# A graph, attention and expert layer on one core: order of transfers, of a branch's pieces, and one-hots and mixer operations given to POOL

## What is computed

```
xn  = layernorm(x)
q,k,v = xn @ Wq,Wk,Wv ;  e = edge_attr @ We            (8 heads of 32)
alpha = <q[dst], k[src] + e> / sqrt(32)
w   = softmax of alpha over the edges of one dst
gnn = segment_sum((v[src] + e) * w, dst) + xn @ Wskip
mix = linear attention over all nodes (phi(q) kv / z) @ Wo,
      layernorm, relu(. @ W1) @ W2, layernorm
x   = x + gnn + mix
x   = x + sum over 8 experts of gate * MLP_e(layernorm(x))
```

## Time and profile before

| | us |
|---|---|
| median of 3 runs | 3732.03 |
| lowest, highest | 3723.98, 3732.52 |
| the profiled execution | 3703.33 |
| its span | 3701.4 |
| PE busy | 3241.8 (88%) |
| DVE busy | 2927.2 (79%) |
| ACT busy | 1719.3 (46%) |
| POOL busy | 1259.3 (34%) |

### The profile page before, as it was taken

The page is one execution under the profiler, slowest core; times in us unless marked ns, Lnnn a source line. Parts: engine busy times, 40 slices in busy tenths (PEclk is TensorE's granted clock), DMA queues, the critical chain, the costliest instruction groups (busy, mean ns, idle before and its releaser), DMA issues.

```text
span 3701.4 us, 72350 instructions
## 1 busy us (share of the span) xinstructions
PE 3241.8 (88%) x17312; PEld 2525.9 (68%) x17312; DVE 2927.2 (79%) x6394; ACT 1719.3 (46%) x4685; POOL 1259.3 (34%) x1313
## 2 busy tenths in 40 slices
PE   4998899999999899999999177777768999999999
PEld 3775566666666666666666145555558999999999
DVE  6776898898888888888888888888856666666665
ACT  1222333333333333333333156666646777777776
POOL 1223666666666666666664021111100000000000
PEclk9998999999999999999999599999979999999999
DMA  7336988898888988888888256666610000000000
GB/s 177 116 115 172 243 250 238 234 249 242 243 245 238 245 237 244 244 246 239 245 238 222 91 173 207 206 207 206 207 60 12 12 17 11 17 11 17 11 17 9
DMA packets 520911, 593.54 MB, mean 160 GB/s; under 512 B 187937, under 2 KB 396979, under 8 KB 520319
## 3 DMA queue, kind: packets, MB, share of 16 engines
q1 hardware_dynamic: 312408, 351.02, 32.7%
q0 software_dynamic: 201888, 232.77, 24.1%
q10 hardware_dynamic: 6409, 7.46, 0.6%
HBM read 426.91 MB, written 163.17 MB: 159 GB/s over the span
## 4 chain that ended last, share of the span: by engine, by line
PE 52%; DVE 18%; issue 13%; SPq 5%; DMA 3%; DVEq 3%; ACT 3%; ACTq 2%; another core or an unknown queue 0%
PE psum L635 10%; PE psum L637 10%; PE psum L636 10%; PE psum L713 6%; PE psum L697 5%; DMA region_s<-ab_d 3%; DVE weights L1373 3%; DVE part L1387 3%; PE psum L849 3%; PE psum L770 2%; DVE region_s L1572 2%; DVE region_x L1560 1%; ACTq L1088 1%; ACT region_s L1083 1%; DVEq L1563 1%
## 5 line engine op out<-in xcount | busy, mean ns | idle before, releaser
L600 POOL DMA_INDIRECT weights<-kv_tab,idx x450 | 547.7, 1217 | 351.9 <-ACT idx L1006 192.1
L1012 ACT ACTIVATE weights<-psum,region_s 125x250 f32<-125x250 f32 x450 | 211.7, 471 | 951.2 <-PE psum L713 524.6
L697 PE MATMUL psum<-we,weights 64*125 64x256 f32 x1800 | 578.4, 428 | 6.5 <-issue 3.4
L849 PE MATMUL psum<-region_s 125*125 125x264 f32 x1800 | 453.9, 401 | 128.8 <-DVE region_s L1572 128.8
L713 PE MATMUL psum<-region_x,weights 125*125 x1800 | 546.9, 429 | 0.0
L1129 ACT ACTIVATE region_s<-psum,bns 128x250 f32<-128x250 f32 x800 | 403.4, 555 | 287.2 <-PE psum L637 287.2
L1622 DVE TENSOR_TENSOR parts_h<-region_s,parts_h 128x500 fp32r<-128x500 f32 x400 | 269.9, 679 | 312.4 <-ACT parts_h L1133 283.1
L849 PEld LDWEIGHTS psum<-region_s 125*125 125x125 f32 x1800 | 304.6, 188 | 277.9 <-issue 152.7
L713 PEld LDWEIGHTS psum<-region_x,weights 125*125 125x125 f32 x1800 | 320.3, 198 | 190.2 <-issue 159.6
L600 POOL DMA_INDIRECT kv_more<-kv_tab,idx x300 | 364.2, 1214 | 142.6 <-issue 102.0
L697 PEld LDWEIGHTS psum<-we,weights 64*125 64x125 f32 x1800 | 291.2, 190 | 163.2 <-issue 148.0
(11 more groups left out here) (246 smaller groups left out, 7628.2 us busy)
## 6 DMA issues: line engine op xcount, KB each, us to landing
region_s<-ve_d SPq DMA_DIRECT2D x450, 256.0 KB, 2.9
ve_d<-weights SPq DMA_DIRECT2D x225, 256.0 KB
ve_d<-kv_more SPq DMA_DIRECT2D x150, 256.0 KB
weights<-in_attr_t SPq DMA_DIRECT2D x450, 62.5 KB
ve_d<-region_r SPq DMA_DIRECT2D x75, 256.0 KB
kv_tab<-region_s SPq DMA_DIRECT2D x50, 224.0 KB
region_s<-ab_d SPq DMA_DIRECT2D x450, 1.0 KB
weights<-kv_tab,idx POOLq DMA_INDIRECT x450
```

What stands on the lines that cost most here:

```text
L600: nc.gpsimd.indirect_dma_start(kg[r][0:T, w, :], None, kv_tab, bass.IndirectOffsetOnAxis(idx[:, r, w:w + 1], 0)).then_inc(gathered[r], 16)
L697: last = mm(psum[0:T, s % 2, w * D:(w + 1) * D], att_b[:, s % RP, w * T:(w + 1) * T], we[:, :], start=True, stop=True)
L849: last = mm(bank, hot[:, s, w, :], pv[:, s, w, 0:PV], start=(w == 0), stop=(w == 1))
```

## The change

- SP loads the dst rows of step k+3 in step k (`AHEAD`), as the first thing of the step, ahead of the store and the attribute load; it has a second set of registers for that, loaded every six steps as well. The first three loads stand ahead of the loop.
- PE's `qprod` stands ahead of `eproj` and `spread` in a step. The branch's pieces of PE are placed anew: "attend", "turn" and "out" one step later, "up" at steps 4 to 7 and 9 to 12, and "down" spread over six steps, of which two lie in the next block (`last_at`). "up" of the pairs 1 to 3 uses one PSUM bank, and waits for the relu of the pair just before.
- ACT's pieces move with them. DVE's "attend" stands at step 4, "norm2" at 3.
- DVE's gain1, gain2 and add2 are done by POOL, at steps 1, 9 and 11 of later blocks, with two new semaphores.
- DVE's register loads stand behind the first large operation of their step, in both loops.
- In the sums pass DVE makes the one-hot of step 0, ACT those of 1, 3 and 5, and POOL those of 2 and 4, with one comparison for each of the two tiles.
- Two semaphores are merged into others.

```diff
-BY_DVE = {0: 1, 3: 2}
-BY_ACT = {1: 1, 2: 2, 4: 3, 5: 4}
+BY_DVE = {0: 1}
+BY_ACT = {1: 1, 3: 2, 5: 3}
+BY_POOL = {2: 1, 4: 2}
...
+            sp.load(ab_regs, walk[0:1, 0, 0:SU])
+            for s in range(AHEAD):
+                load_ab(s, s, ab_regs[s])
...
                     if s % SU == 0:
                         sp.load(regs, walk[0:1, 0, bass.ds(k, SU)])
+                        sp.load(ab_regs, walk[0:1, 0, bass.ds(k + AHEAD, SU)])
+                    if k + AHEAD < STEPS:
+                        load_ab(k + AHEAD, (s + AHEAD) % SB, ab_regs[s % SU])
...
-                    load_ab(k, s, regs[s % SU])
...
+            def gain1(b):
+                pool.wait_ge(m_x1, b + 1)
+                nc.gpsimd.tensor_tensor(my[:, b % 2], mx1, row2(R_G1), ALU.mult).then_inc(m_g1, 1)
+            def gain2(b):
+                pool.wait_ge(m_x2, b + 1)
+                order(nc.gpsimd.tensor_tensor(mx2[:, :, :], mx2[:, :, :], row2(R_G2), ALU.mult))
+            def add2(b):
+                pool.wait_ge(m_res_in, (b + 1) * 32)
+                nc.gpsimd.tensor_tensor(mout[:, :, :], mx2[:, :, :], mres[:, :, :], ALU.add).then_inc(m_outr, 1)
...
+                    if s == 1 and b >= 1:
+                        gain1(b - 1)
+                    if s == 9 and b >= 2:
+                        gain2(b - 2)
+                    if s == 11 and b >= 2:
+                        add2(b - 2)
...
+                        order(placed)
+                        for w in range(2):
+                            compared = nc.gpsimd.tensor_scalar(hot[:, s, w, :], iota[:, :], place_in[:, s, w:w + 1], None, ALU.is_equal)
+                        compared.then_inc(hot_pool, 1)
...
-                    if n == 4 and not (isinstance(b, int) and b == NB - 1):
-                        pe.wait_ge(m_an, b + 2)
                     if o == 0 and pair >= 2:
-                        pe.wait_ge(m_hr, b * 4 + pair - 1)
+                        pe.wait_ge(m_hr, b * 4 + pair)
...
-            mix_at = {2: ("q", 0), 3: ("q", 1), 7: ("attend",), 10: ("turn",), 11: ("out", 0), 12: ("out", 1)}
-            late_at = {1: ("turn1",), 3: ("up", 0), 4: ("up", 1), 5: ("up", 2), 6: ("up", 3), 10: ("up", 4), 11: ("up", 5),
-                       12: ("up", 6), 13: ("up", 7), 14: ("down", 0, 3), 15: ("down", 3, 7), 16: ("down", 7, 11), 17: ("down", 11, 16)}
+            mix_at = {2: ("q", 0), 3: ("q", 1), 8: ("attend",), 11: ("turn",), 12: ("out", 0), 13: ("out", 1)}
+            late_at = {1: ("turn1",), 4: ("up", 0), 5: ("up", 1), 6: ("up", 2), 7: ("up", 3), 9: ("up", 4), 10: ("up", 5),
+                       11: ("up", 6), 12: ("up", 7), 14: ("down", 0, 3), 15: ("down", 3, 6), 16: ("down", 6, 9), 17: ("down", 9, 12)}
+            last_at = {0: ("down", 12, 14), 1: ("down", 14, 16)}
...
                     if some:
+                        qprod(k - LAGQ, (s - LAGQ) % SB, regs[s % SU])
                         eproj(k - LAGQ, (s - LAGQ) % SB, b * (SB // RP) + (s - LAGQ) // RP + 1, 0)
...
-                        qprod(k - LAGQ, (s - LAGQ) % SB, regs[s % SU])
...
-            mix_at, late_at = {1: "phi", 8: "turn", 17: "turn1"}, {2: 0, 4: 1, 9: 2, 11: 3}
+            mix_at, late_at = {1: "phi", 9: "turn", 17: "turn1"}, {3: 0, 5: 1, 8: 2, 10: 3}
...
-            mix_at = {0: "phi", 3: "attend", 8: "sum1", 9: "stats1", 10: "root", 11: "root2", 12: "norm1", 13: "gain1"}
+            mix_at = {0: "phi", 4: "attend", 8: "sum1", 9: "stats1", 10: "root", 11: "root2", 12: "norm1"}
             late_at = {15: "sum2", 16: "stats2", 17: "root"}
-            last_at = {1: "root2", 4: "norm2", 5: "gain2", 6: "add2"}
+            last_at = {1: "root2", 3: "norm2"}
...
                     add_edges(k, s, b * (SB // RK) + s // RK + 1)
+                    if s % SU == 0:
+                        dve.load(regs, walk[0:1, 2, bass.ds(k, SU)])
                     multiply(k, s)
```

More of the change, by code:

```diff
@@ L58 @@
 LAGS = 2
+AHEAD = 3
 LAGP = 2
@@ L464, in _ @@
             regs = [sp.alloc_register(f"sp_pair{s}") for s in range(SU)]
+            ab_regs = [sp.alloc_register(f"sp_ab{s}") for s in range(SU)]
             def load_ab(k, s, reg):
@@ L605, in _ @@
                 b_body(b)
+            gain1(NB - 1)
+            for b in (NB - 2, NB - 1):
+                gain2(b)
+                add2(b)
+            order.reset()
             pool.wait_ge(back, CT)
@@ L611, in d_body @@
             def d_body(it):
-                for s in BY_ACT:
+                for s in range(SU):
+                    if s in BY_DVE:
+                        continue
                     k = it * SU + s
@@ L802, in b_body @@
                         eproj(k - LAGQ, (s - LAGQ) % SB, b * (SB // RP) + (s - LAGQ) // RP + 1, 1)
-                        qprod(k - LAGQ, (s - LAGQ) % SB, regs[s % SU])
+                    if s in last_at and not (isinstance(b, int) and b < 2):
+                        mix(b - 2, u, last_at[s])
                     if s in late_at and not (isinstance(b, int) and b == 0):
@@ L815, in _ @@
                 eproj(STEPS - LAGQ + s, SB - LAGQ + s, (STEPS - LAGQ + s) // RP + 1, 1)
-                qprod(STEPS - LAGQ + s, SB - LAGQ + s, regs[s])
-            for g in late_at.values():
+                if s in last_at:
+                    mix(NB - 2, 1, last_at[s])
+            for g in (*late_at.values(), *last_at.values()):
                 mix(NB - 1, 0, g)
@@ L1035, in mix @@
                         n = 2 * pair + o
-                        last = fn(mh[:, n, :], psum[:, 5 + pair % 2, o * BN:(o + 1) * BN], ACT.Relu,
+                        last = fn(mh[:, n, :], psum[:, 5 if pair == 0 else 6, o * BN:(o + 1) * BN], ACT.Relu,
                                   bias=cols[:, C_B1 + n:C_B1 + n + 1])
                     last.then_inc(m_hr, 1)
-            mix_at, late_at = {1: "phi", 8: "turn", 17: "turn1"}, {2: 0, 4: 1, 9: 2, 11: 3}
+            mix_at, late_at = {1: "phi", 9: "turn", 17: "turn1"}, {3: 0, 5: 1, 8: 2, 10: 3}
             def b_body(b, u):
@@ L1421, in mix @@
                 elif g == "norm1":
+                    wait(dve, m_g1, b)
                     signal(norm_apply(my[:, u], mx1), m_x1, b + 1)
-                elif g == "gain1":
-                    order(tt(my[:, u], mx1, row2(R_G1), ALU.mult))
                 elif g == "root":
@@ L1453, in b_body @@
                     k = b * SB + s
-                    if s % SU == 0:
-                        dve.load(regs, walk[0:1, 2, bass.ds(k, SU)])
                     if s in last_at and not (isinstance(b, int) and b < 2):
@@ L1562, in d_body @@
             def d_body(it):
-                dve.load(regs, walk[0:1, 1, bass.ds(it * SU + LAGQ - LAG, SU)])
                 for s in range(SU):
@@ L1573, in d_body @@
                        pv[:, s, :, D:PV].unsqueeze(3).broadcast_to((T, 2, H, C)), ALU.mult).then_inc(pv_ready, 1)
+                    if s == 0:
+                        dve.load(regs, walk[0:1, 1, bass.ds(it * SU + LAGQ - LAG, SU)])
                     if s >= LAG or not (isinstance(it, int) and it == 0):
```

41 lines of the change are left out of this document (24 added, 17 removed).

## The result

| us | before | after |
|---|---|---|
| median (4 runs each, on one chip) | 3732.28 | 3600.72 |
| lowest to highest | 3723.98 to 3742.75 | 3597.34 to 3612.18 |
| profiled execution, its span | 3703.33, 3701.4 | 3612.18, 3610.2 |

The ratio is 0.9652, 95% interval 0.9619 to 0.9684: 132 us less by the medians. The forecast was 3607. The two traces differ by only 91 us, since the profiled execution of before was 21 us under the lowest of its four runs and that of after was the slowest of its four.

The account below looks back on a forecast made before the run. PE and DVE, coupled step by step, were taken to bound the edge stage, DVE the sums pass. Blocks of 63.7 us save 100, iterations of 7.3 save 25: 3732 - 125 = 3607 us, range 3520 to 3692.

Parts of the forecast that it names:

- What bounds the kernel: Edge stage: PE and DVE coupled through two PSUM banks, unequal steps costing more than either sum; sums pass: DVE.
- The first list of pairs: Edge stage before: larger of PE's step s+5 and DVE's step s, added over 18 steps, given as 64.8 us a block.
- Part 1: Edge stage: dst rows three steps sooner are never late; the whole 76.7 us and most of the 29.9 go.
- Part 2: Edge stage: levelled branch brings the pairs to 62.9, 1.9 us less a block; DVE waits up to 2 for "out".
- Part 3: Edge stage: with DVE's register load behind the add, some 2 of 3.2 us of waiting a block go.
- Part 4: Edge stage: three operations on POOL, hidden there, each holding DVE 0.4 us, 1.2 us a block.
- Part 5: Sums pass: one one-hot and part of a load gap leave DVE, comparisons cost 0.47; iteration 7.3 us, 25 us saved.
- A: Edge stage: dst-row load was hidden anyway, only DVE's relief of 51 us comes, sums pass gives nothing: 3681; chance 0.22.
- B: Both stages reach their floors, 60 us a block and 6.83 an iteration: 3482; chance 0.15.
- D: Both stages: the moves cancel (wait at "out", shared bank for "up", comparison near 0.74 us): 3732; chance 0.08.
- C: Both stages: the port decides, POOL operations wait out multiplies and hold DVE, slower: about 3806; chance 0.10.

Follow-up runs that it names:

- edge_only: The changed kernel with the sums pass of before, so only the edge-stage edits: 3675.55 us, ratio to before 0.9860.
- no_level: The changed kernel with PE's old order in a step and the branch's old places: 3597.00 us, ratio to before 0.9658.
- nopm_noload: no_poolmix with DVE's register load of the edge stage ahead of the add again: 3582.67 us, ratio to before 0.9622.
- ahead_sums: The kernel before with only the early dst rows and the two sums-pass edits: 3584.13 us, ratio to before 0.9603.
- store_first: The changed kernel with SP's store ahead of the dst rows and one register load of nine, not two of six: 3606.86 us, ratio to before 0.9689.
- ahead_only: The kernel before with only the dst rows loaded three steps sooner: 3651.13 us, ratio to before 0.9792.
- no_poolmix: The changed kernel with gain1, gain2 and add2 back on DVE: 3560.07 us, ratio to before 0.9567.
- pool_memset: no_poolmix with four POOL memsets, which read no SBUF, in each place of the three operations: 3566.38 us, ratio to before 0.9587.

## Why the prediction was right, step by step

The total was right (125 us foreseen, 132 measured) by terms that made up for each other; that it came within 7 us is luck. The sums pass gave 43 us more than foreseen, the edge stage 50 less. The 100 us of the edge stage were 2.9 us a block for stalls and slow clock (72 us; the dst rows and DVE's register loads share this term), 1.9 for the new positions (48), less 0.8 for the waits that they bring (20). The runs give 60 to 74 for the rows and 16 to 23 for the register load, nothing for the positions, and take 32 to 41 for POOL's operations; edge_only, with all of them, gave 50.

- **What bounds the kernel**: right for the sums pass (DVE), half right for the edge stage. That PE's and DVE's steps pair off, with the larger of each pair as the price, is not borne out. The first list of pairs adds to 64.6 as printed, not 64.8. Recounted from the two lists, some 0.5 of the 1.9 us a block is DVE's relief (the pairs where gain2 and gain1 stood), and levelling alone is 1.2 to 1.4 us, 30 to 35 us in all. Levelling measured nothing twice (no_level against after, nopm_noload against ahead_sums), to within some 20 us.
- **Part 1, dst rows**: the edit was worth what was foreseen, the way was half right. The load is gone from the waits, the spread idles 26.8 us (foreseen under 30), and no price of the second register load shows (store_first). But "the whole 76.7 and most of the 29.9 go" is true of that row only: in all PE idles as long as before (124 and 128 us in before and ahead_only), now for DVE, and the gain in the traces is PE's work at a higher clock. So that 60 to 74 us lie near the 76.7 of the row is in part luck.
- **Part 2, levelling**: the term that failed. The foreseen wait at "out" came (24.3 us) and was free; the 1.9 us a block did not come. The one-hot is ready in time, as foreseen (5.8 us of waiting for ACT against 24.6), but PE waits for DVE instead, before its query. The granted clock is 0.96, short of the 0.98 foreseen.
- **Part 3, DVE's load**: mechanism right, size off. Norm1's 42.4 us of idle time are 0.0; 16 to 23 us came of 50.
- **Part 4, POOL's mixer operations**: the sign was wrong. The hold was priced well: 1.29 us an operation as foreseen, and 35.7 us over the 71 operations up to the last step is 0.50 each where I took 0.4. (The row that it rests on was misread: the DVE operation of the earlier trace rows ends at 73.89, not with POOL's at 73.61. That it took 0.96 us is right.) The prediction let slack between the pairs absorb most of this hold, and that failed; the relief of DVE, 51 us of busy time, was worth next to nothing beside it. That a relief is taken up by the ring and the two banks, while a hold of 2 us falls into one step, is argued and not shown. Why the price (32 to 41 us) is as large as the whole sum of the holds isn't shown. The granted clock differs too, 0.97 with them and 1.00 without in the two inner windows; what part it has is open.
- **Part 5, sums pass**: 68 us for 25. A comparison takes 0.95 us (median) and never less than 0.588. The median lies above my upper end of 0.74, and the least above my 0.35 and the 0.38 estimated beside it. Yet the multiplies are not pushed apart, where I charged 0.47 an iteration. Without that charge my sum was 6.83; measured are 6.79. The overlap took its toll from POOL, which has the time: 395 us busy of 509.
- **Rivals**: A's price fell with ahead_only, though the turn of stalls into waits for DVE is real. B's floor of 6.83 came in the sums pass, its 60 us a block did not: from the first to the last spread a block takes 66.7 us in before, 65.5 in after and 63.4 in no_poolmix. D, the moves cancelling, holds for the edge stage's edits beside the dst rows, not for the whole. C fell; its mechanism (POOL's turn holds DVE) is real in the edge stage and absent in the sums pass.

The edge stage shows DVE's small add ending with POOL's operation every time it was held, and pool_memset shows no hold. The Trainium skill, SBUF — State Buffer, section "SBUF: two separate sides", says as much: a Vector operation with two SBUF inputs and a GpSimd operation that reads SBUF lock each other out, and whichever starts second waits for the whole of the first. The start times of the edge stage do not fit its last part, as 17 of the 30 held adds were recorded as started first. Nor do the sums pass's multiplies: they have two SBUF inputs, POOL's comparisons read SBUF, and only the comparisons were stretched.

## What to carry to other kernels

Before work goes from DVE to POOL, look at which operations of DVE run beside it: beside a two-operand POOL operation a 0.165 us add took up to 2.2 us, while comparisons with one tensor input held nothing in a pass where POOL had time to spare. A transfer of 5.5 us, issued two to three steps of 3.7 us ahead, showed as the wait before one instruction, and was worth nearly its row once it was issued earlier. Ask all the same where that idle time goes: here it came back as waits for another engine, and the gain showed in PE's clock. Sums of step costs by pairs, with banks and rings between the engines, promised what no run gave; take an engine's relief as zero until the profile shows that engine ending the waits.

## What was not expected of the hardware

- A small add of DVE can start 0.1 to 0.9 us ahead of the POOL operation and still end with it (17 of the 30 held ones; at 1022.68 it was 0.67 ahead, four times its own length). POOL's operation seems to hold DVE from before its recorded start; why isn't known.
- POOL's comparison of 125 columns takes 588 ns unhindered, nearly the 741 of a two-operand operation of 256 columns, and 1365 at most beside multiplies.
- Without POOL's three operations the clock granted through the inner edge stage was 1.00 at 1408 us of PE busy in 1500; with them 0.97 at 1395.
